# Four low parts of b subtracted on GpSimd, and a chunk's turn and steps made beside the weights' chain

## What is computed

```python
mask = (jnp.arange(Lq) < length[:, None])
u_m = u * mask[:, None, :]                                   # u is x: (B=64, H=64, L=1024)
dtA = A * dt[:, None];  Cs = Cc * (jnp.exp(dtA) - 1.0) / A   # A, C complex, N=64 modes a head
kernel = 2.0 * jnp.einsum('hn,hnl->hl', Cs, jnp.exp(dtA[:, :, None] * jnp.arange(Lq))).real
y = irfft(rfft(u_m, 2L) * rfft(kernel, 2L))[..., :Lq] + u_m * D[:, None];  y = y * mask[:, None, :]
scores = y @ Wr.T;  gates = softmax(top 16 of 64 scores);  G = gates put back at their experts
h = jnp.einsum('nd,krd->nkr', y, A_ffn)                      # K=64, R=16: "a", 1024 x 1024
out = x + 2.0 * jnp.einsum('nkr,kdr->nd', h * G[:, :, None], B_ffn)   # "b", 1024 x 1024
```

## Time and profile before

| | us |
|---|---|
| median of 3 runs | 898.14 (897.69 to 899.48) |
| the profiled execution, its own time | 898.15 |
| its span in the trace | 896.3 |
| TensorE busy | 881.5 (98%) |
| VectorE busy | 753.8 (84%) |
| ScalarE busy | 371.6 (41%) |
| GpSimd busy | 7.5 (1%) |

### The profile page before, as it was taken

One profiled execution on the slowest core, in us unless ns is written; L12 is line 12 of the kernel. 1 busy time (PEld: TensorE's weight loads), 2 busy tenths in 40 slices (PEclk: granted clock), 3 DMA queues, 4 the chain that ended last, 5 costly groups with the idle time before them and its releaser, 6 DMA issues.

```text
span 896.3 us, 15701 instructions
## 1 busy us (share of the span) xinstructions
PE 881.5 (98%) x4488; PEld 783.0 (87%) x4488; DVE 753.8 (84%) x2580; ACT 371.6 (41%) x629; POOL 7.5 (1%) x24
## 2 busy tenths in 40 slices
PE   6999999999999999999999999999999999999998
PEld 4667998998899998899998889998889999889997
DVE  7899998888898888898888888888889888888722
ACT  5663554444542353543344443344453344442100
POOL 3000000000000000000000000000000000000000
PEclk9999999999999999999999999999999999999999
DMA  7631315444454444454433354434345444445331
GB/s 231 243 53 54 77 30 126 111 116 112 124 140 117 110 111 114 109 140 117 124 109 110 102 140 126 117 108 114 109 128 140 115 97 114 123 114 141 100 95 48
DMA packets 81415, 103.32 MB, mean 115 GB/s; under 512 B 30628, under 2 KB 63460, under 8 KB 81396
## 3 DMA queue, kind: packets, MB, share of 16 engines
q1 hardware_dynamic: 80868, 102.63, 42.1%
q0 software_dynamic: 160, 0.10, 0.2%
q10 hardware_dynamic: 368, 0.36, 0.1%
HBM read 67.34 MB, written 34.93 MB: 114 GB/s over the span
## 4 chain that ended last, share of the span: by engine, by line
PE 91%; DVE 4%; ACT 1%; issue 1%; DMA 1%; POOL 1%; SPq 0%; DVEq 0%; POOLq 0%; ACTq 0%
PE out_ps L1360 25%; PE h_ps L1360 18%; PE out_ps L1364 12%; PE h_ps L1364 9%; PE turn_ps L1360 8%; PE turn_ps L1364 4%; PE conv_ps L1316 2%; PE conv_ps L1317 2%; PE conv_ps L1318 2%; PE conv_ps L1289 1%; PE conv_ps L1326 1%; PE conv_ps L1290 1%; PE conv_ps L1327 1%; PE conv_ps L1328 1%; PE conv_ps L1291 1%; PE h_ps L1369 1%
## 5 line engine op out<-in xcount | busy, mean ns | idle before, releaser
L1360 PE MATMUL out_ps<-b_lo,g_hi 128*128 128x512 f32 x496 | 196.2, 395 | 0.0
L1360 PE MATMUL out_ps<-b_hi,g_hi 128*128 128x512 f32 x496 | 194.7, 393 | 0.0
L1360 PE MATMUL h_ps<-a_hi,y_hi 128*128 128x384 f32 x480 | 161.4, 336 | 0.0
L1360 PE MATMUL h_ps<-a_lo,y_hi 128*128 128x384 f32 x480 | 161.4, 336 | 0.0
L1364 PE MATMUL out_ps<-b_hi,g_lo 128*128 128x512 f32 x496 | 122.7, 389 | 0.3 <-DVE g_lo L1040 0.3
L564 ACT ACTIVATE g_hi<-square_sb 128x1024 fp32r<-128x1024 f32 x28 | 29.7, 1061 | 220.4 <-DMA square_sb<-moved 210.8
L1360 PEld LDWEIGHTS out_ps<-b_lo,g_hi 128*128 128x128 f32 x496 | 93.2, 188 | 21.2
L1364 PEld LDWEIGHTS out_ps<-b_hi,g_lo 128*128 128x128 f32 x496 | 93.0, 188 | 20.8 <-DVE g_lo L1040 0.8
L1360 PEld LDWEIGHTS out_ps<-b_hi,g_hi 128*128 128x128 f32 x496 | 93.0, 188 | 20.0 <-ACT g_hi L557 0.6
L820 DVE SCALAR_TENSOR_TENSOR z<-swapped,step_other,part 128x64 f32<-128x64 f32 x384 | 92.3, 281 | 12.5 <-DVE swapped L815 0.7
L813 DVE SCALAR_TENSOR_TENSOR part<-z,step_own,conv_ps 128x64 f32<-128x64 f32 x384 | 90.4, 277 | 9.7 <-POOL step_other L435 1.3
(11 more groups left out here) (232 smaller groups left out, 1442.4 us busy)
## 6 DMA issues: line engine op xcount, KB each, us to landing
xt_in<-in_xt SPq DMA_DIRECT2D x32, 512.0 KB, 4.2
x_in<-in_x SPq DMA_DIRECT2D x62, 256.0 KB, 3.8
out<-x_in SPq DMA_DIRECT2D x62, 256.0 KB, 3.1
moved<-square_sb SPq DMA_DIRECT2D x28, 512.0 KB, 8.6
square_sb<-moved SPq DMA_DIRECT2D x112, 128.0 KB, 2.9
b_in<-in_b_t SPq DMA_DIRECT2D x8, 512.0 KB, 6.7
a_in<-in_a_t SPq DMA_DIRECT2D x8, 512.0 KB, 9.0
moved_in<-square_in SPq DMA_DIRECT2D x26, 128.0 KB, 2.8
```

What stands on the lines that cost most here:

```text
L1360: pe.matmul(o, hi[:, c, :], moving[:, c, columns], start=first and c == order[0] and moving is w_hi, stop=False)
```

## The change

Four pieces of `b` get their low part from GpSimd (`BY_POOL`: pieces 5, 6, 3, 2), three stay with VectorE (`BY_DVE`: 7, 1, 0), one (piece 4) with TensorE and ScalarE. GpSimd makes `far_turn` as soon as `turns` is there, no longer after `powers`, and makes the steps in front of its four DMAs. ScalarE takes `far_sin` ahead of `sines(0)`, `low_weights` behind it, the high parts of pieces 3 and 2 behind `decays(1)`, and `theta(2)` inside `first_step`. VectorE makes states of chunks 1 and 2 of tile 1 in a row. TensorE runs four filling products in place of `whole_b(1)`.

```diff
+        BY_POOL = [EARLY[1], MIDST[0], MIDST[2], MIDST[3]]
+        BY_DVE = [MIDST[1], MIDST[4], MIDST[5]]
...
             pool.wait_ge(s_turns, 1)
-            pool.wait_ge(s_powers, 1)
             pool.tensor_scalar(far_turn[:, 1, :], turns[:, :], float(P), None, ALU.mult).then_inc(s_away_turn, 1)
...
-            pool.wait_ge(s_kdone, 1)
-            for i in range(HT):
-                for block, source in first_rows(i, range(JM // 2, JM)):
-                    pool.dma_start(block, source).then_inc(s_tpool[i], 16)
             pool.wait_ge(s_farwave, 2)
...
             pool.tensor_scalar(step_other[:, :], far_turn[:, 1, :], sign[:, :], -1.0, ALU.mult, ALU.mult).then_inc(s_steps, 1)
+            pool.wait_ge(s_kdone, 1)
+            for i in range(HT):
+                for block, source in first_rows(i, range(JM // 2, JM)):
+                    pool.dma_start(block, source).then_inc(s_tpool[i], 16)
+            for i in BY_POOL:
+                pool.wait_ge(s_whi, HIGH.index(i) + 1)
+                _, arrived, hi, lo = loads[i]
+                pool.tensor_tensor(out=lo, in0=arrived, in1=hi.bitcast(F32), op=ALU.subtract).then_inc(s_wpool, 1)
...
             theta(0)
-            low_weights(0)
+            act.wait_ge(s_far, 1)
+            act.activation(far_sin[:, :, :], far_turn[:, :, :], ACT.Sin, scale=TWO_PI).then_inc(s_farwave, 1)
             sines(0)
+            low_weights()
             split_weights(EARLY[1])
             copy_k(0)
             whole_in(0, in_ps)
-            act.wait_ge(s_far, 1)
-            act.activation(far_sin[:, :, :], far_turn[:, :, :], ACT.Sin, scale=TWO_PI).then_inc(s_farwave, 1)
             theta(1)
-            low_weights(1)
             for i in MIDST[:2]:
                 split_weights(i)
             sines(1)
             decays(1)
-            theta(2)
-            split_weights(MIDST[2])
+            for i in MIDST[2:4]:
+                split_weights(i)
...
                 whole_in(1, in_ps_1)
+                theta(2)
                 exps(0)
-                for i in MIDST[3:]:
+                for i in MIDST[4:]:
                     split_weights(i)
...
-            for i in MIDST[:2]:
-                low_weights(i)
+            low_weights(BY_DVE[0])
             make_powers(1)
...
                 sum_gates()
-                for i in MIDST[2:5]:
-                    low_weights(i)
+                low_weights(BY_DVE[1])
                 first_states(1)
-                states(1, range(1, 2))
+                states(1, range(1, 3))
                 add_skip(1)
                 gate_part(0, 2)
                 low_gated(0, 0)
-                low_weights(MIDST[5])
-                states(1, range(2, 4))
+                low_weights(BY_DVE[2])
+                states(1, range(3, 4))
...
-            whole_b(0)
-            for n in range(11):
-
-                pe.matmul(h_ps[:, 0, 0:P], ident[:, :], ident[:, :], start=True, stop=True)
+            whole_b()
+            keep_on(11)
             weighed_row()
             turn_in(0)
             whole_feed(0)
-            whole_b(1)
+            keep_on(4)
```

More of the change, by code:

```diff
@@ L204, in build @@
             sem(n) for n in ("s_mask", "s_rates", "s_tanh", "s_turns", "s_sins", "s_far", "s_farwave"))
-        s_whi, s_wlo = sem("s_whi"), sem("s_wlo")
+        s_whi, s_wlo, s_wpool = sem("s_whi"), sem("s_wlo"), sem("s_wpool")
         s_theta, s_whole, s_args, s_sine, s_decay, s_powers, s_other, s_raw = (
@@ L235, in build @@
         LATE = list(range(FIRST_B))
-        REST_PS = [turn_ps, h_ps]
+        BY_POOL = [EARLY[1], MIDST[0], MIDST[2], MIDST[3]]
+        BY_DVE = [MIDST[1], MIDST[4], MIDST[5]]
         HIGH = EARLY + MIDST + LATE
@@ L442, in split_weights, with low_weights @@
                 act.activation(hi, arrived, ACT.Copy).then_inc(s_whi, 1)
-            def low_weights(n):
-                act.wait_ge(s_rest_ps, n + 1)
-                _, _, _, lo = loads[EARLY[n]]
+            def low_weights():
+                act.wait_ge(s_rest_ps, 1)
+                _, _, _, lo = loads[EARLY[0]]
                 for half in range(2):
-                    act.activation(lo[:, half * HALF:(half + 1) * HALF], REST_PS[n][:, half, :], ACT.Copy).then_inc(s_blo, 1)
+                    act.activation(lo[:, half * HALF:(half + 1) * HALF], turn_ps[:, half, :], ACT.Copy).then_inc(s_blo, 1)
             def theta(t):
@@ L1255, in _, with whole_b, keep_on @@
         def _(pe):
-            def whole_b(n):
-                _, arrived, hi, _ = loads[EARLY[n]]
-                pe.wait_ge(s_whi, n + 1)
+            def whole_b():
+                _, arrived, hi, _ = loads[EARLY[0]]
+                pe.wait_ge(s_whi, 1)
                 for half in range(2):
                     columns = slice(half * HALF, (half + 1) * HALF)
-                    pe.matmul(REST_PS[n][:, half, :], ident[:, :], arrived[:, columns], start=True, stop=False)
-                    last = pe.matmul(REST_PS[n][:, half, :], minus[:, :], hi[:, columns], start=False, stop=True)
+                    pe.matmul(turn_ps[:, half, :], ident[:, :], arrived[:, columns], start=True, stop=False)
+                    last = pe.matmul(turn_ps[:, half, :], minus[:, :], hi[:, columns], start=False, stop=True)
                 last.then_inc(s_rest_ps, 1)
+            def keep_on(count):
+                for n in range(count):
+                    pe.matmul(h_ps[:, 0, 0:P], ident[:, :], ident[:, :], start=True, stop=True)
             def turn_in(t, target=in_ps):
@@ L1373, in up @@
                     if first:
-                        pe.wait_ge(s_wlo, len(MIDST) + n + 1)
+                        pe.wait_ge(s_wlo, len(BY_DVE) + n + 1)
                     if n == 1 and conv:
@@ L1395, in first_step @@
                 pe.wait_ge(s_w[0], 16)
-                pe.wait_ge(s_blo, 2 * len(EARLY))
                 for c in range(NC // 2):
@@ L1421, in first_step @@
                 pe.wait_ge(s_kcopy, 2)
-                pe.wait_ge(s_wlo, 2)
+                pe.wait_ge(s_wpool, 2)
+                pe.wait_ge(s_wlo, 1)
                 down_high(0, (4, 5, 6, 7), first=True)
@@ L1427, in first_step @@
                 pe.wait_ge(s_ghi, 2)
-                pe.wait_ge(s_wlo, len(MIDST))
+                pe.wait_ge(s_wpool, len(BY_POOL))
+                pe.wait_ge(s_wlo, len(BY_DVE))
                 down_high(0, (0, 1, 2, 3))
```

## The result

| | before | after |
|---|---|---|
| median, 6 runs each (us) | 897.89 (897.69 to 899.48) | 901.66 (901.21 to 903.59) |
| ratio of after to before | | 1.0039 (1.0029 to 1.0050) |
| span of the profiled execution | 896.3 | 899.6 |
| tile-1 convolution starts | 52.22 | 55.74 |
| from there to the span's end | 844.1 | 843.9 |

The changed kernel is 0.4% slower. The forecast was 898.3 us, with 895.4 to 900.4 as its range: it fell outside. The last two lines of the table say where the time lies. The block behind `whole_conv(1)` kept its length, and its start moved by 3.52 us. So the frame of the prediction stands for this pair, and the whole question is what happened in the first 55 us.

The account below looks back on a forecast made before the run. TensorE was taken as the bound, a fixed block behind the tile-1 convolution's start. Gates 2.8 us later through holds, less 2.67 us saved on VectorE, put that start 0.13 us later: 898.15 + 0.13 = 898.3 us, range 895.4 to 900.4.

Parts of the forecast that it names:

- the frame: From 52.2 us on TensorE is a fixed block of 843.8 us that slides; only the tile-1 convolution's start can move.
- The gain without a collision: With no hold that matters, TensorE reaches the tile-1 convolution at 49.66 us: 2.56 us gained, 895.6 us; chance 0.25.
- 0.34 us of standing for a high part: Between gates and last `part`: VectorE's wait of 0.34 us was to go with two removed subtractions worth 2.33 us.
- That VectorE is held: VectorE's instructions beside GpSimd's stand until GpSimd's instruction is over; taken as likelier, 7 in 10.
- The price of a piece: One GpSimd subtraction of 1024 columns takes 2.3 us, with ends of 1.2 and 3.7 us.
- Step 1: GpSimd's turn and step products beside VectorE's small instructions from 9.4 us: holds make VectorE 0.85 us later.
- Step 2: GpSimd's piece 5, 20.05 to 22.35 us, holds VectorE's first `z` product: it and TensorE's `whole_product` 1.05 us later.
- Step 3: GpSimd's piece 6, 25.5 to 27.8 us: a `z` product waits 0.75 us, hidden because TensorE wants the last state later.
- Step 4: GpSimd's pieces 3 and 2, from 35.55 us: piece 3 holds one `out_raw` line, so the gates start 2.8 us later.
- Step 5: VectorE's last `part` ends at 52.08 + 2.8 - 2.67 = 52.21 us, so the tile-1 convolution starts 0.13 us later.
- the term 2.67: VectorE's saving between gates and last `part`: two subtractions worth 2.33 us plus 0.34 us of standing.
- Rival (b): Holds with a slow GpSimd: at 3.7 us a piece 902.4 us, deciding from 3.0 us a piece; chance 0.1.

Follow-up runs that it names:

- e7: Changed kernel with each GpSimd subtraction cut into eighths, each waiting for the end of the one before; tile-1 convolution starts at 49.56 us.
- e12: Third run of the changed kernel with waiting eighths on GpSimd; convolution starts at 49.81 us, ratio 0.9974 to the kernel before.
- e9: Second run of the changed kernel with waiting eighths on GpSimd; convolution starts at 50.65 us, ratio 0.9974 to the kernel before.
- e3: Changed kernel with GpSimd's four subtractions replaced by memsets, leaving those low parts out; convolution starts at 50.41 us, ratio 0.9966 to the kernel before.
- e4: Changed kernel with each GpSimd subtraction cut into eight of 128 columns in a row, without waits; convolution starts at 52.09 us, ratio 0.9986 to the kernel before.
- e10: The changed kernel itself, run once more; convolution starts at 54.35 us, ratio 1.0054 to the kernel before.
- e8: Changed kernel with GpSimd making only pieces 3 and 2, in waiting eighths, VectorE the others; convolution starts at 50.19 us, ratio 0.9979 to the kernel before.
- e5: Changed kernel with GpSimd making only pieces 5 and 6, whole, VectorE the others; convolution starts at 53.04 us, ratio 0.9987 to the kernel before.

## Why the prediction was wrong

**The frame** (a fixed block behind the tile-1 convolution) was right for these two traces: 844.1 against 843.9 us. The experiments' traces, 845.4 to 856.8 us, show that the block isn't fixed everywhere.

**The gain without a collision** was about right: 49.66 us was worked out for the start, e7 measured 49.56 and e12 49.81. That e7 agrees to 0.1 us is luck, since e9 with the same code gave 50.65 and all three still have small holds. One term beside it was wrong. The "0.34 us of standing for a high part" isn't there: of before's three subtractions behind the gates none waited, they ran 3.41 us without a break. After has one of them, which takes 1.14 us (44.41 to 45.55). So two are worth 2.27 us, not 2.67.

```profile
38.63 3.48 DVE L858 TENSOR_TENSOR b_lo<-b_in,b_hi 128x1024 fp32r<-128x1024 f32 x3
42.04 0.34 DVE L802 COPY z<-conv_ps 128x64 f32<-128x64 f32 x2
```

**That VectorE is held** was right in kind. The Trainium skill's rule (SBUF — State Buffer, "Who interferes with whom"), that a two-input VectorE instruction and a GpSimd instruction that reads exclude each other, and that one which only writes does not, is what the `z` rows of after and of e3 show. That the block is over with the first instruction is not what e4 shows at one place: 2.41 us through eighths of 0.45.

**The price of a piece** was right: 2.3 us, measured 2.36.

**Step 1** (the turn beside the weights' chain) was too dear: 0.85 us, measured 0.18 (`powers` of tile 0 at 14.69 instead of 14.51). GpSimd's small instructions took the stretch instead, `step_own` 0.77 us where its neighbour took 0.41.

**Step 2** (piece 5) came in the place and kind written, `z` held to 22.3 us, and TensorE's L1350 waited 1.4 us. It cost less: with GpSimd's DMAs 0.4 us ahead of what was written, `whole_product` began at 24.87 us, 0.47 later than before, not 1.05.

**Step 3** (piece 6) failed in after, as a result of step 1. With VectorE 0.7 us earlier than I had it, the `z` pair was just in flight when the piece began, and was held for all of it: 2.12 us, not 0.75. I had called it hidden. It wasn't: `y_m` of chunks 1 to 3 stands behind this pair in VectorE's queue, and TensorE waited 0.9 us for it. My working looked only at the last state, not at what is queued behind the held instruction. In e10 the same hold was 0.78 us, TensorE didn't wait for `y_m`, and the start was 1.39 us earlier: that is what step 3 cost.

**Step 4** (pieces 3 and 2) is the step that failed in both traces, and the largest part of the miss. It had one of the two `out_raw` lines held, by one piece. Both were: the tensor_scalar L730 by piece 3, and then the scalar_tensor_tensor L734 by piece 2, which started as soon as piece 3 was over. 2.15 + 2.11 us instead of some 2.3. The prediction knew that tensor_scalar-like instructions are held, from the cast row, and still let it pass freely. (The prediction's L730 is L734 in the changed kernel, whose L730 is the tensor_scalar.) The gates came at 43.28, 5.78 us late, where 2.8 was written: 4.26 us of these two holds, and 1.51 because `powers` came late, nearly all of it from step 3. In e10, where step 3 went as written, they came at 41.89, 4.39 late: the same 4.26 and 0.13.

**Step 5** followed with the gates: 5.78 - 2.27 = 3.51 us, the measured 3.52. So the 3.39 us between the forecast start (52.35) and the measured one (55.74) are, up to rounding, 1.39 of step 3, 1.59 of step 4 (4.39 for 2.8) and 0.40 of the term 2.67. With e10's phase the start, 54.35 us, would by the frame have given 900.3 us, just inside the range. That the range was missed is in part chance; that step 4 was wrong is not.

**Rival (b)**, slower than before, named the right outcome for a wrong reason. It made a slow GpSimd responsible, "as soon as a piece takes 3.0 us". At 2.36 us two pieces in a row did it. The rival that was missing is: the two back pieces hold one after the other.

## What to carry to other kernels

Work moved from VectorE to GpSimd is not beside VectorE but in front of it, wherever VectorE's instructions read two tensors from SBUF while GpSimd reads, or are a tensor_scalar like `out_raw`'s. Count one hold for each GpSimd instruction, also for those that follow one another without a gap, and with it everything that stands behind the held instruction; a hold (here 2.1 us) can be dearer than the work taken away (1.16 us). If GpSimd must help, cut its work into short instructions that wait for each other, so that VectorE gets in between: the same work went from 7.95 us of holds to 1.9.

## What the runs showed of the hardware

- A hold can last longer than the GpSimd instruction that began it: 2.41 us through a queue of 0.45 us instructions (e4, one place), but at most 0.28 us for a VectorE instruction once each eighth waits for its predecessor (e7, e8, e9, e12).
- A GpSimd memset of 1024 columns (0.95 to 1.00 us) left two pairs of the two-input `z` at 0.48 us and made a pair of tensor_scalar 0.77 us longer (e3).
- `part`, a scalar_tensor_tensor with one of its two tensor inputs in PSUM, wasn't held: 0.46 us at 25.68 us in e5, in the middle of GpSimd's piece 6 (25.08 to 27.45), as elsewhere. `z`, with both in SBUF, was held behind it at 26.47.
- The hold is mutual: a GpSimd eighth took 1.43 us instead of 0.45 beside VectorE's subtraction (e4, 40.18 to 41.50 us).
- The phase of two engines (which of them starts first, by tenths of a microsecond) decides over a hold of 0.78 or 2.12 us with the same code (after and e10), which is 1.4 us of the start.
- In e9 TensorE's granted clock was 0.50 from 18.8 to 20.5 us, after 1.18 and 0.53 us of standing. With 0.90 (e7) and 1.15 us (e5) of standing at the same place it stayed at 1.00.
